# Layer 3 of a three-layer graph convolution gathers rows as three BF16 parts that layer 2 makes tile by tile

## The reference

```python
src = jnp.concatenate([edge_index[0], loops])      # loops: every node to itself
dst = jnp.concatenate([edge_index[1], loops])
deg = segment_sum(ones, dst); dinv = rsqrt(deg)
norm_edge = dinv[src] * dinv[dst]
for W, b in ((W1, b1), (W2, b2), (W3, b3)):        # 256->512, 512->512, 512->256
    h = relu(segment_sum((h @ W)[src] * norm_edge[:, None], dst) + b)
out = layernorm(x + h)
```

## Time and profile before

| | |
|---|---|
| profiled execution, its span | 2421.05 us, 2419.3 us |
| PE busy | 2217.9 us (92%) |
| POOL busy | 1699.1 us (70%) |
| DVE, ACT busy | 997.9 us (41%), 718.6 us (30%) |
| DMA | 508.70 MB, mean 210 GB/s |

### The profile page before, as it was taken

The page is one execution under the profiler, slowest core; times in us unless marked ns, Lnnn a source line. Parts: engine busy times, 40 slices in busy tenths (PEclk is TensorE's granted clock), DMA queues, the critical chain, the costliest instruction groups (busy, mean ns, idle before and its releaser), DMA issues.

```text
span 2419.3 us, 33202 instructions
## 1 busy us (share of the span) xinstructions
PE 2217.9 (92%) x10765; PEld 1488.0 (62%) x10765; DVE 997.9 (41%) x1154; ACT 718.6 (30%) x1501; POOL 1699.1 (70%) x1767
## 2 busy tenths in 40 slices
PE   6977799999999998899999999899998799999998
PEld 6855577767777774444444444444444488888886
DVE  8888333333333313343444434443422233333433
ACT  6711222323333321232222223132221233333332
POOL 5177777777777766777777777777777766666663
PEclk9889899999999999999999999999999999999999
DMA  7346666667676666788777888778787655567773
GB/s 221 128 128 201 203 204 205 201 199 207 209 210 210 207 191 204 243 244 250 243 237 242 250 249 244 235 243 250 239 263 231 189 174 171 169 177 211 216 218 95
DMA packets 219959, 508.70 MB, mean 210 GB/s; under 512 B 38444, under 2 KB 106915, under 8 KB 219827
## 3 DMA queue, kind: packets, MB, share of 16 engines
q0 software_dynamic: 117216, 365.08, 51.6%
q1 hardware_dynamic: 83955, 109.08, 13.3%
q10 hardware_dynamic: 18656, 32.75, 4.3%
HBM read 433.60 MB, written 73.16 MB: 209 GB/s over the span
## 4 chain that ended last, share of the span: by engine, by line
PE 53%; POOL 15%; issue 14%; DMA 7%; DVE 6%; POOLq 3%; ACT 1%; DVEq 0%; ACTq 0%; SPq 0%
POOL rows L736 15%; PE ps_acc L1664 9%; PE ps_d L1664 8%; PE ps_h L1752 7%; PE ps_o L1713 6%; PE ps_T L1752 6%; PE ps_acc L1660 5%; DMA rows<-table,idx 5%; PE ps_d L1763 5%; POOLq L745 2%; PE ps_h L1704 2%; PE ps_d L1616 2%; DMA rows<-table_parts,idx 1%; PE ps_e L1734 1%; PE ps_l L1734 1%
## 5 line engine op out<-in xcount | busy, mean ns | idle before, releaser
L736 POOL DMA_INDIRECT rows<-table,idx x1249 | 1201.6, 962 | 461.5 <-issue 367.4
L1664 PE MATMUL ps_acc<-rows,sel 128*128 128x512 f32 (+2 forms) x1496 | 602.8, 519 | 79.2 <-DMA rows<-table,idx 55.8
L953 DVE SCALAR_TENSOR_TENSOR sel<-ps_e,firsts,dstT 128x1152 f32<-128x1152 f32 (+1 forms) x214 | 302.7, 1415 | 796.9 <-PE ps_acc L1664 307.3
L736 POOL DMA_INDIRECT rows<-table_parts,idx x483 | 456.8, 946 | 156.4 <-issue 141.0
L1664 PE MATMUL ps_d<-rows,sel 128*128 128x512 f32 (+2 forms) x1190 | 512.0, 541 | 42.2 <-DMA rows<-table,idx 41.9
L1664 PEld LDWEIGHTS ps_acc<-rows,sel 128*128 128x128 f32 x1496 | 274.7, 197 | 247.7 <-issue 144.6
L1664 PEld LDWEIGHTS ps_d<-rows,sel 128*128 128x128 f32 x1190 | 210.9, 190 | 193.6 <-issue 120.1
L1660 PE MATMUL ps_acc<-rows,sel 128*128 128x256 bf16 (+1 forms) x1533 | 243.6, 276 | 32.6 <-DMA rows<-table_parts,idx 17.3
L1713 PE MATMUL ps_o<-low,hT 128*128 128x512 f32 (+1 forms) x784 | 271.8, 490 | 0.9 <-ACT hT L1361 0.9
L1752 PE MATMUL ps_T<-pairs_r,rows_r 128*128 128x512 f32 x686 | 229.2, 450 | 9.6 <-ACT rows_r L1443 5.7
L1763 PE MATMUL ps_d<-big 128*128 128x256 bf16 x1470 | 227.3, 273 | 0.0
(11 more groups left out here) (190 smaller groups left out, 1729.4 us busy)
## 6 DMA issues: line engine op xcount, KB each, us to landing
rows<-table,idx POOLq DMA_INDIRECT x1249, 3.8
table<-made SPq DMA_DIRECT2D x49, 256.0 KB, 3.4
acc<-table SPq DMA_DIRECT2D x49, 256.0 KB, 4.2
built<-big SPq DMA_DIRECT2D x30, 384.0 KB
low<-built ACTq DMA_DIRECT2D x30, 384.0 KB
built_bytes<-big SPq DMA_DIRECT2D x54, 192.0 KB
low<-built_bytes ACTq DMA_DIRECT2D x54, 192.0 KB
table_parts<-big SPq DMA_DIRECT2D x24, 384.0 KB
```

The source lines that it names most:

```text
L736: pool.indirect_dma_start(out=to, out_offset=None, in_=its[0:nodes, :], in_offset=bass.IndirectOffsetOnAxis(ap=idx[:, of, k:k + 1], axis=0 ...
L953: v.scalar_tensor_tensor(to[:, k:k + FRONT, :], numbers.unsqueeze(1).broadcast_to([P, FRONT, P]), firsts[:, bass.ds(t, 1)], dstT[:, bass.d ...
L1664: return mm(to[:, 0:w], sel[:, k, :], rows_of[phase][:, k, 0:w] if first is None else first, start=start, stop=stop)
```

## The change

Layer 3's windows gather from a new table of three BF16 parts. Layer 2 makes the parts tile by tile. For tile t, ACT writes the top part from PSUM (`keep_top`), DVE takes the rest into PSUM (`take_rest`), ACT writes the middle part (`keep_mid`), DVE the lowest (`take_lowest`), and SP stores the three (`store_parts`). POOL waits between the layers for these stores. `take_apart` now works on one tile at a time, in every window from the third on. The ring of widened counts moves from the row buffers to the place of the weights W2 and W3, and the loaded counts have four buffers, one for each piece, instead of two of a whole tile. A piece is loaded again right after it was widened, one dense tile ahead; the four loads between the layers go. The rounds of layer 2 have 12 windows instead of 14, so the same builds lie in 36 windows without a break and not in 36 of the first 42.

```diff
-    ROUND, STARTS = 14, (0, 3, 5, 7, 10, 12)
+    ROUND, STARTS = 12, (0, 2, 4, 6, 8, 10)
+        RING_AT = W3_AT + KH * C - 2 * RING * P
+        ring = [low_words_r[:, RING_AT + b * RING * P:RING_AT + (b + 1) * RING * P]... for b in range(2)]
+        split = [away[...][:, 0:PARTS * C]..., sb("split", [P, PARTS, C], BF16)[:, :, :]]
+        ps_rest = ps_h[:, 0:C]
+                    def store_parts(t):
+                        sp.wait_ge(parts_ready, t + 1)
+                        sp.dma_start(table_parts[2][bass.ds(t * P, P), :], split[t % 2]...).then_inc(parts_stored, 16)
                             own_rows(t)
+                            store_parts(t - 2)
                             stores(i, o, first)
                             store(t - 1, nth(1, t - 1))
...
+                        store_parts(T - 2)
                         store(T - 1, nth(1, T - 1))
+                        store_parts(T - 1)
-                        pool.wait_ge(stored, 16 * (T * phase - 1))
+                            pool.wait_ge(parts_stored, 16 * (T - 1))
+                        window(phase, nth_of_windows(phase, 0), WINDOWS[phase] % 2, None, LATE, in_parts=phase == 2)
-            def take_apart(turn, t, n):
+            def take_apart(t):
+                v_.wait_ge(stored, 16 * (nth(1, t) + 1))
+                if t in FREE_OF_MAKING:
+                    v_.wait_ge(tile_stored[FREE_OF_MAKING.index(t)], 16 * len(PIECES) * (DENSE // 2 + 1))
+                v.tensor_copy(high_r[:, t, :], whole[:, t, :]).then_inc(highs_ready, 1)
+                v_.wait_ge(highs_ready, t + 1)
+                v.tensor_tensor(low_r[:, t, :], whole[:, t, :], high_r[:, t, :], ALU.subtract).then_inc(pairs_ready, 1)
+            def take_rest(t):
+                v_.wait_ge(top_ready, t + 1)
+                if t > 0:
+                    v_.wait_ge(parts_ready, t)
+                v.tensor_tensor(ps_rest, whole[:, t, :], split[t % 2][:, 0, :], ALU.subtract).then_inc(rest_ready, 1)
+            def take_lowest(t):
+                v_.wait_ge(mid_ready, t + 1)
+                v.tensor_tensor(split[t % 2][:, 2, :], ps_rest, split[t % 2][:, 1, :], ALU.subtract).then_inc(parts_ready, 1)
                         steady(1, ROUND * i + o + 1, (WINDOWS[1] + o + 1) % 2, hots, complete)
-                        if o == 2 and not first:
-                            take_apart(i - 1, n * (i - 1), n)
+                            take_rest(t - 2)
+                            take_apart(t - 3)
+                            take_lowest(t - 2)
+            def keep_top(t):
+                if t >= 2:
+                    act.wait_ge(parts_stored, 16 * (t - 1))
+                nc.scalar.activation(split[t % 2][:, 0, :], ps_o[:, 0:C], ACT.Copy, scale=dinv[:, t:t + 1]).then_inc(top_ready, 1)
+            def keep_mid(t):
+                act.wait_ge(rest_ready, t + 1)
+                nc.scalar.activation(split[t % 2][:, 1, :], ps_rest, ACT.Copy).then_inc(mid_ready, 1)
                     keep(0, PAIRS // 2)
+                    if per == 1 and 1 <= t < T - 1:
+                        keep_mid(t - 1)
                     act.wait_ge(turned, s + 1)
...
                 make(phase, t, s, per)
+                if phase == 1 and per == 1:
+                    keep_top(t)
+                    if t >= T - 2:
+                        keep_mid(t)
             def widen(g, x, more=True):
-                act.wait_ge(blocks_in[d % 2], 16 * len(PIECES) * (DENSE_OF // 2 * g + d // 2 + 1))
+                act.wait_ge(blocks_in[piece], 16 * (j + 1))
...
-                    load_blocks(DENSE_OF * g + d + 2, d % 2, piece)
+                    load_blocks(j + 1, piece)
-                for piece in range(len(PIECES)):
-                    load_blocks(1, 1, piece)
                 widen(0, 0)
-                if first and d == 0 and h in [t0 for t0, _ in PAIRS_OF]:
+                if first and d == 0:
+                    pe.wait_ge(pairs_ready, h + 1)
-                    steady(2, GROUP * g + b, LAST_PLACES[2], with_dense(g, b, first), ps=ps_sums[odd])
+                    steady(2, GROUP * g + b, LAST_PLACES[2], with_dense(g, b, first), ps=ps_sums[odd], in_parts=True)
```

More of the change, by code:

```diff
@@ L407, in gnn_program @@
         x_parts_stored = sem("x_parts_stored")
-        blocks_in = [sem(f"blocks_in{b}") for b in range(2)]
+        blocks_in = [sem(f"blocks_in{b}") for b in range(len(PIECES))]
         late_ready = sem("late_ready")
@@ L660, in phases @@
                             own_rows(t)
+                            store_parts(t - 2)
                             stores(ROUNDS, o)
                             store(t - 1, nth(1, t - 1))
-                        with sp.Fori(ROUND * ROUNDS + 3, T) as t:
-                            rows_and_store(t, nth(1, t - 1))
+                        for t in range(ROUND * ROUNDS + 3, T):
+                            own_rows(t)
+                            store_parts(t - 2)
+                            store(t - 1, nth(1, t - 1))
+                        store_parts(T - 2)
                         store(T - 1, nth(1, T - 1))
+                        store_parts(T - 1)
                     elif per > 1:
@@ L1216, in one_window @@
                            (q, place_of(q, False), q % 2) if t == ROUND * ROUNDS + 1 else None, last=t == T - 1)
[L1217 to L1225, removed]
+                    take_rest(t - 2)
+                    take_apart(t - 3)
+                    take_lowest(t - 2)
+                take_apart(T - 3)
                 to_next(1)
-                t0, t1 = PAIRS_OF[-1]
-                v_.wait_ge(stored, 16 * 2 * T)
-                take_apart(len(PAIRS_OF) - 1, t0, t1 - t0)
+                take_rest(T - 1)
+                take_lowest(T - 1)
+                take_apart(T - 2)
+                take_apart(T - 1)
                 def finish_gathered(g, b):
@@ L1238, in behind @@
                     t = GROUP * g + b + 1
-                    steady(2, t, odd, last=last, dense=(g, b))
+                    steady(2, t, odd, last=last, in_parts=True, dense=(g, b))
                     finish_gathered(g, b)
@@ L1544, in pieces @@
                         for x in xs:
-                            widen(g, x, not (last and x >= 2 * len(PIECES)))
+                            widen(g, x, not (last and x >= (DENSE_OF - 1) * len(PIECES)))
                     if not first:
@@ L1811, in first_window @@
                     ps = ps_sums[n % 2]
-                    slots(phase, n, ORDER[:-1], rows_of[phase][:, 0, 0:WIDTH[phase]], None, beside, ps)
+                    in_parts = phase == 2
+                    first = rows_parts[:, 0, :] if in_parts else rows_of[phase][:, 0, 0:WIDTH[phase]]
+                    slots(phase, n, ORDER[:-1], first, None, beside, ps, in_parts)
                     if phase == 1:
```

87 lines of the change are left out of this document (54 added, 33 removed).

## The result

The changed kernel takes **2383.46 us** (median of four runs, 2382.98 to 2385.16) against 2421.8 us for the kernel before in the same comparison (four runs, 2417.82 to 2422.99). The ratio is 0.9845, with a 95% interval from 0.983 to 0.9861. It is faster by 1.55%; forecast were 2386.0 us and a range from 2370 to 2413. The span of the profiled execution fell from 2419.3 to 2383.3 us, by 36.0 us.

The account below looks back on a forecast made before the run. POOL's gathers were taken to bound layer 2 and PE layer 3; -36.8 + 5.1 - 6 + 1 + 2 = -34.7 from 2421.05 gave 2386 us, with a range of 2370 to 2413.

Parts of the forecast that it names:

- Slots: Layer 3 on PE: three BF16 matmuls replace two FP32 ones, 0.327 us instead of 0.43 for each of 357 slots; -36.8 us.
- Uncovered waits: Layer 3: faster PE waits longer for widenings, 0.31 us at six group starts, 0.46 at seven fourth tiles; +5.1 us.
- Small pieces: Layer 2: tile-sized `take_apart` frees gathers of 12.5 us, three new small DVE operations a tile cost 6.7; net -6 us.
- Work beside layer 2: Layer 2: added ACT, DVE and SP work and denser builds stay hidden behind POOL's pace; 0, or +15 if cover failed.
- Loads of counts: Lead shrinks from two dense tiles to one, some 17 us, against a few us to land; 0.
- Between the layers: Seam before layer 3: POOL starts later, near 1918, PE's first dense matmul stays near 1925.5; +1 us, between -1 and +5.
- DMA in layer 3: Late layer 3: rows of 1.5 KB raise DMA's share to 0.88 or 0.94; late rows cost +2 us, 0 to 8.
- Rival 1: Late layer 3: DMA becomes the bound at a share of 0.79, +29 in place of +2, 2413 us; chance 0.10.
- Rival 2: Layer 3: float32r weight loads stand open behind BF16 matmuls, 0.080 us at each of 357 slots, +29, 2415 us; chance 0.06.
- Rival 3: Layer 2: small DVE operations hold POOL for their whole length, +7.8 in all, 2429 us, slower; chance 0.06.
- Rival 4: Layer's edge or layer 2: something gives the gain back, ending within 0.2% of before; chance 0.05.

Follow-up runs that it names:

- Experiment 7: Changed kernel with layer 3's slots in twos, dense matmuls of two places issued together in front of every second slot; 2378.78 us, ratio 0.9838.
- run 9: The changed kernel unaltered, measured again as base for later runs on the same chip; 2381.68 us, ratio 0.9853 to the kernel before.
- run 6: Changed kernel with ACT widening ahead of the deviations at a group's start and before the fourth tile; 2370.44 us, ratio 0.981.
- experiment 3: Changed kernel with `take_apart` in six large pieces again (12, 12, 8, 8, 6, 3 tiles); 2392.13 us, ratio 0.9901.
- 2: Changed kernel with layer 3's slots in FP32 again and the parts neither made nor stored; 2405.83 us, ratio 0.9967.
- 4: Changed kernel with `take_rest` (two operands from SBUF) done four times for each tile; 2385.92 us, ratio 0.9878.
- 10: Changed kernel with six further DVE operations a tile, 294 in all, both operands from SBUF; 2391.65 us, ratio 0.9892.
- 5: Changed kernel with `take_lowest` (one operand from SBUF, one from PSUM) done four times for each tile; 2379.06 us, ratio 0.9836.
- 11: Changed kernel with six further DVE operations a tile, 294 in all, one operand from PSUM; 2382.54 us, ratio 0.9854.
- run 1: Changed kernel with layer 3's slots in FP32 again, gathering from `table2`, parts still made and stored; 2409.6 us, ratio 0.9974.

## Why the prediction was right, step by step

**Slots, forecast -36.8 us: the mechanism held, the size was too large.** Measured are -30.9 us, 0.087 us for each of 357 slots and not 0.103. What a slot costs stands in PE's timeline, from one slot's start to the next. The kernel before, with three and then four dense matmuls between:

```profile
2003.86 0.59 PE L1664 MATMUL ps_d<-rows,sel 128*128 128x256 f32 x2
2004.10 1.04 PE L1752 MATMUL ps_T<-pairs_r,rows_r 128*128 128x512 f32 x3
2004.98 0.59 PE L1664 MATMUL ps_d<-rows,sel 128*128 128x256 f32 x2
2005.23 1.27 PE L1752 MATMUL ps_T<-pairs_r,rows_r 128*128 128x512 f32 x4
2006.34 0.59 PE L1664 MATMUL ps_d<-rows,sel 128*128 128x256 f32 x2
```

And the changed kernel:

```profile
2004.86 0.50 PE L1721 MATMUL ps_d<-rows,sel 128*128 128x256 bf16 x3
2005.12 0.94 PE L1813 MATMUL ps_h<-pairs_r,low_words_r 128*128 128x512 f32 x3
2005.90 0.50 PE L1721 MATMUL ps_acc<-rows,sel 128*128 x3
2006.16 1.18 PE L1813 MATMUL ps_h<-pairs_r,low_words_r 128*128 128x512 f32 x4
2007.17 0.50 PE L1721 MATMUL ps_acc<-rows,sel 128*128 128x256 bf16 x3
...
2029.61 1.17 PE L1813 MATMUL ps_T<-pairs_r,low_words_r 128*128 128x512 f32 x4
2030.63 0.50 PE L1721 MATMUL ps_d<-rows,sel 128*128 128x256 bf16 x3
2030.89 0.71 PE L1813 MATMUL ps_T<-pairs_r,low_words_r 128*128 128x512 f32 x2
2031.73 0.47 PE L1813 MATMUL ps_h<-pairs_r,low_words_r 128*128 128x512 f32 x1
...
2053.08 0.50 PE L1813 MATMUL ps_T<-pairs_r,low_words_r 128*128 128x512 f32 x1 [1.25 <-ACT low_words_r L1506]
```

With three dense matmuls the period fell from 1.12 to 1.04 us, with four from 1.36 to 1.27: 0.08 to 0.09. A dense matmul takes 0.231 us in the median, so a slot in parts takes 1.04 - 3 x 0.231 = 0.347 us, where the prediction took layer 1's 0.327. The step that failed is "whether the neighbour is a slot, a dense tile or FP32 work": the neighbour matters a little. The first BF16 matmul starts 0.239 us behind a float32r one, the next 0.120 behind it, against 0.231 and 0.109 between their like. Experiment 7 took out about half of the changes and PE's work fell by 3.2 to 3.6 us, 0.02 us for each of 168 slots that no longer stand alone; within its pairs the second slot's BF16 matmuls follow at 0.109 throughout. So the changes of type cost it; what in the engine does so stays open.

**Uncovered waits, forecast +5.1; measured +2.7 net.** At a group's start the wait went from 0.95 to 1.25 us, the last row above: +0.30 at each of six, as worked out (0.31). At the fourth tile the widening was in time to 0.2 us; now the row at 2031.73 above, the tile's first matmul, starts 0.53 us behind the one before it (the second of the two in the row at 2030.89, at 2031.20); where nothing was late this was 0.23 to 0.26, so about 0.3 us are new, at each of seven places (0.24 to 0.32). Sized at 0.46, it is less in part because each slot gave less: 4.5 slots at 0.087 are 0.39. From start to start the two kinds of wait cost 3.9 us more than before. The idle time grew by 2.7 only, because most of the wait at a fourth tile is counted as busy: the records of the two matmuls in front last until 2031.60.

PE's busy time holds something else that changed. At layer 3's start, behind an idle time of 3.91 us before and 3.79 now, the granted clock is 0.50, the level of 1.2 GHz, and then 1.00. The stage view, before and then now:

```profile
1924.80:1931.50 6.70, 6.02 (x14) 4.80 (x15) 1.52 (x2) 2.07 (x2) 4.59 (x6) 0.50 0.76 241
...
1917.60:1920.80 3.20, 3.20 (x10) 2.00 (x9) 0.31 (x1) 1.49 (x1) 2.59 (x3) 0.50 0.91 262
```

In layer 3 this is some 6.1 us before and 3.5 now, of which PE loses half: 1.3 us less now. No step of the change explains that, and it isn't steady: in run 9, the same kernel, the stretch has 4.0 us of layer 3, and in run 6 6.2. It happens to cancel the 1.2 us of waits that are counted as busy, so that the 0.087 us for a slot stand.

Experiment 6 shows that both waits come from ACT's order: with the order changed, 7.0 us of idle time went.

**Small pieces, forecast -6; measured -7.3** in the lengths of gathers (784 of them lie 12.4 us above 946 ns, the median before, and now 5.1) and -8.0 in layer 2's duration. Of the 5.1, some 2.3 are no disturbance: in this one trace every gather is 3 ns longer (minimum 945 and not 942, median 949 and not 946). In run 9, the same kernel, the sum is 4.6. All three parts held: the large pieces cost some 11 us (experiment 3), the new operations cost little (2, 4, 10), and an operation with a PSUM operand costs nothing (5, 11). The price of 0.053 us for an operation with two SBUF inputs was high; 10 gives 0.025 to 0.034. Length alone does no harm: in the changed kernel's layer 2 the longest operations of `one_hots` last 3.4 us, with one operand from PSUM, and no gather beside them takes over 1.17 us. A long copy, with one SBUF input and an output to SBUF, does harm: the gather beside the copy of 1.75 us took 2.12. DVE's group now, and POOL before:

```profile
L1156 DVE TENSOR_TENSOR low<-ps_e,lo 128x3136 bf16<-128x3136 f32 x36 | 123.0, 3416 | 0.0
...
1262.86 2.12 POOL L736 DMA_INDIRECT rows<-table,idx  x1 [0.30 <-issue]
```

**Work beside layer 2, forecast 0.** Held: POOL's waits for PE there are 10.7 us, against 11.6. **Loads of counts, forecast 0.** Held, and more than that: in ACT's group of widenings in layer 3 no idle time is put down to a load, where it was 33.3 us or more before. A widening then waited for all four pieces of its tile, and now waits for its own. The group before, and then now:

```profile
L1443 ACT ACTIVATE rows_r<-low 128x1536 fp32r<-128x1536 uint8 (+1 forms) x111 | 167.4, 1508 | 159.2 <-PE ps_T L1752 57.3 <-PE ps_h L1752 55.1 <-DMA low<-built_bytes 33.3
...
L1506 ACT ACTIVATE low_words_r<-low 128x1536 fp32r<-128x1536 uint8 (+1 forms) x111 | 167.5, 1509 | 135.5 <-PE ps_T L1813 66.6 <-PE ps_h L1813 64.9 <-issue 2.3
```

**Between the layers, forecast +1; measured +1.9, and most of it is the clock's.** POOL's timeline there:

```profile
1899.27 0.94 POOL L758 DMA_INDIRECT rows<-table,idx  x1 [0.30 <-issue]
1907.29 0.95 POOL L758 DMA_INDIRECT rows<-table_parts,idx  x1 [7.07 <-DMA table_parts<-split]
```

And SP's:

```profile
1898.75 0.43 SPq L569 DMA_DIRECT2D table_parts<-away  x1
1899.22 0.43 SPq L563 DMA_DIRECT2D table<-big  x1
1904.53 0.32 SPq L569 DMA_DIRECT2D table_parts<-split  x1
```

The two stores do follow each other: the parts of tile 47 are issued at 1904.53, when its `table2` rows have landed, and POOL starts at 1907.29, 8.0 us behind its last gather, where it was 3.8. PE doesn't feel this, its first rows are there. What it feels is ACT's chain from the last `make` to the first dense matmul, 3.78 us before and 3.66 after, equal as worked out, and the end of the last window. PE's timeline there, before and after, and the stage view of the second:

```profile
1913.14 3.70 PE L1664 MATMUL ps_d<-rows,sel 128*128 128x512 f32 x8 [0.96 <-DMA rows<-table,idx]
...
1903.45 5.40 PE L1725 MATMUL ps_d<-rows,sel 128*128 128x512 f32 x8 [2.10 <-DMA rows<-table,idx]
...
1903.90:1907.10 3.20, 3.20 (x5) 1.35 (x4) 0.00 (x0) 0.00 (x0) 0.00 (x0) 0.50 0.22 79
```

The same eight matmuls take 1.7 us longer: behind a wait of 2.10 us their granted clock is 0.50, the level of 1.2 GHz, and before it was 1.00. They start 4.2 us behind POOL's last gather and not 3.9, because rows landed 0.3 us later. The three stores beside them are not shown to be the cause: run 1 makes the same stores there, and has 3.8 us. In run 9, the same kernel as here, the seam is 18.0 us too, but the half clock falls on `product` instead, whose eight matmuls take 3.13 us and not 1.99. Whether the change makes such stretches likelier was not tested; in runs 3 and 10 none falls into the seam, and it is 16.7 and 16.4 us. So the forecast +1 came near, but not by its own terms.

**DMA in layer 3, forecast +2; measured 0.** The share late in layer 3 is 0.88 (first fence above, third row), at 281 GB/s; 0.88 to 0.94 was worked out. But PE's groups of slots in layer 3 carry no idle time at all:

```profile
L1721 PE MATMUL ps_acc<-rows,sel 128*128 128x256 bf16 (+1 forms) x558 | 93.7, 277 | 0.0
L1721 PE MATMUL ps_d<-rows,sel 128*128 128x256 bf16 (+1 forms) x510 | 85.3, 276 | 0.0
```

**The rivals.** Rival 1 (DMA) is not seen, by these rows. Rival 2 (weights that stay open, 0.08 us a slot) falls: float32r matmuls still follow each other at 0.231 us, and a change costs 0.02 us, whatever its cause. Rival 3 (short operations hold POOL for their length) falls by 10: 10 us against 127. The Trainium skill ("SBUF — State Buffer", section "SBUF: two separate sides") counts a VectorE operation with two SBUF inputs, beside a GpSimd operation that reads SBUF, among those that take the ports the two share, for the whole instruction. The runs agree as to which operations disturb (10 against 11), and for pieces of 3.36 us as to the length; for operations of 0.43 us they show less than a tenth of it. Rival 4 fell with the sum: nothing gave the gain back.

The steps as measured give -30.9 + 2.7 - 8.0 + 1.9 + 0 = -34.3, where -34.7 was forecast. The mechanisms are those forecast, but that the sum comes so close is luck, for the misses cancel. The slots were 5.9 us too hopeful and the seam 0.9; the waits were 2.4 us too gloomy, DMA 2 and layer 2 another 2. The rest of the 36.0 us of span is mostly layer 1's 1.9, which no step of the change explains.

## What to carry to other kernels

Price a stage by what it waits for: here the same diff was worth 31 us of PE's work in one layer and 8 us of POOL's gathers in another, by two mechanisms that have nothing to do with each other. When the bounding engine gets faster, list the places where it meets a hand-written order of another engine; moving two widenings of each group ahead of a wait gave a further 7 us of 454. And cut a long VectorE operation with two SBUF inputs, or a long copy, into tile-sized ones when indirect gathers run beside it, or let one operand come from PSUM.

## What the runs showed of the hardware that I had not expected

A change between float32r and BF16 matmuls on PE costs about 0.02 us for each slot that stands alone between float32r matmuls, though the matmuls of either kind keep their pace among their like (0.231 and 0.109 us). And the cost of a VectorE operation for the gathers beside it is not proportional to its length: 3.36 us made one gather 2.8 us longer, while 294 of 0.433 us cost 0.025 to 0.034 us each.

At the seam between two layers a few microseconds of TensorE at half clock decide as much as the work that was moved there: 1.7 us of the 1.9 in this trace, at a place that differs from one execution of the same kernel to the next. Before two seams are compared, the granted clock in each is to be read.
